# Cached keys prepared once per page and kept in DRAM, one score pass over 544 keys, masks kept in DRAM

## What is computed

```python
# layer 0: B=32 rows, S=32 tokens, HID=512, D=128, 32 query heads, 8 key heads
q, k, v = x @ Wq.T, x @ Wk.T, x @ Wv.T              # per head of 128
q, k    = rope(rmsnorm(q) , pos), rope(rmsnorm(k), pos)
kc, vc  = k_cache[block_table], v_cache[block_table]  # 16 pages of 32 tokens per row: 512 cached keys
scores  = q @ concat(kc, k).T / sqrt(D)               # 512 + 32 keys
scores  = where(key_index < seqlens or key is new, scores, -1e30)
x       = x + (softmax(scores) @ concat(vc, v)) @ Wo.T
# layer 1: x = x + x @ W.T + 2 * sum over the two best of 8 experts of gate * (x @ A.T) @ B.T
```

## Time and profile before

| | |
|---|---|
| runs | 1477.67, 1478.95, 1482.95 us; median 1478.95 |
| profiled execution, span from first to last instruction | 1451.3 us (the profile gives no own time beside its span; the median of the runs is 27.7 us above it) |
| PE busy (matmul) | 1356.5 us, 93% |
| DVE, ACT, POOL busy | 78%, 53%, 67% |
| mean granted TensorE clock | 0.982 of full speed |
| DMA moved | 188.72 MB, mean 130 GB/s |

### The profile page before, as it was taken

One profiled execution on the slowest core, in us unless ns is written; L12 is line 12 of the kernel. 1 busy time (PEld: TensorE's weight loads), 2 busy tenths in 40 slices (PEclk: granted clock), 3 DMA queues, 4 the chain that ended last, 5 costly groups with the idle time before them and its releaser, 6 DMA issues.

```text
span 1451.3 us, 28498 instructions
## 1 busy us (share of the span) xinstructions
PE 1356.5 (93%) x8640; PEld 1162.0 (80%) x8640; DVE 1132.6 (78%) x2891; ACT 766.9 (53%) x1989; POOL 973.1 (67%) x1269
## 2 busy tenths in 40 slices
PE   2599999998999999999999999999999999999889
PEld 1478888887878888887777888888787888888777
DVE  6688877777887778788877878887888888777754
ACT  1356555555664555556554555666555556555431
POOL 5676777777766677776766777777777777676500
PEclk8699999999999999999999999999999999999999
DMA  6434444454543343436533433445544343435401
GB/s 228 133 87 121 133 119 134 123 173 133 173 117 116 125 119 125 135 108 202 164 117 107 138 112 112 128 125 181 170 142 129 104 129 117 131 122 167 124 22 58
DMA packets 61380, 188.72 MB, mean 130 GB/s; under 512 B 10736, under 2 KB 11504, under 8 KB 58608
## 3 DMA queue, kind: packets, MB, share of 16 engines
q0 software_dynamic: 40960, 134.25, 31.3%
q1 hardware_dynamic: 19504, 53.50, 10.5%
q10 hardware_dynamic: 864, 0.46, 0.1%
HBM read 177.95 MB, written 12.32 MB: 131 GB/s over the span
## 4 chain that ended last, share of the span: by engine, by line
PE 69%; DVE 21%; issue 5%; ACT 2%; DMA 1%; DVEq 1%; POOL 0%; SPq 0%; ACTq 0%; POOLq 0%
PE PROJ L182 13%; PE MISC L182 13%; PE O L359 10%; PE S L182 10%; PE PT L349 8%; PE KT L338 5%; DVE probs L736 4%; PE O L361 3%; DVE scores L729 2%; PE PROJ L328 2%; DVE kT_lo L750 2%; DVE rope_v L703 2%; PE PROJ L330 2%; DVE mask L716 2%; DVE rope_u L699 2%
## 5 line engine op out<-in xcount | busy, mean ns | idle before, releaser
L976 POOL DMA_INDIRECT kv_rows<-in_kv,step_idx x512 | 529.8, 1035 | 219.6 <-issue 117.8
L550 ACT ACTIVATE pT<-PT 128x640 f32<-128x640 f32 x256 | 180.2, 704 | 300.6 <-PE PT L349 300.6
L359 PEld LDWEIGHTS O<-pT,kv_rows 128*128 128x128 f32 x2048 | 262.6, 192 | 27.0 <-ACT pT L550 9.8
L359 PE MATMUL O<-pT,kv_rows 128*128 128x128 f32 x2048 | 274.8, 277 | 2.9 <-ACT pT L550 2.6
L546 ACT ACTIVATE kT_hi<-KT 128x512 fp32r<-128x512 f32 x256 | 151.2, 590 | 225.1 <-PE KT L338 225.0
L750 DVE TENSOR_TENSOR kT_lo<-KT,kT_hi 128x512 fp32r<-128x512 f32 x256 | 176.0, 687 | 71.3 <-ACT kT_hi L546 70.7
L554 ACT ACTIVATE probs<-scores,min_all 128x640 f32<-128x640 f32 x256 | 212.7, 831 | 23.3 <-DVE min_all L729 21.0
L349 PEld LDWEIGHTS PT<-ident,probs 128*128 128x128 f32 x1280 | 142.1, 141 | 89.9 <-DVE probs L736 78.7
L349 PE MATMUL PT<-ident,probs 128*128 128x128 f32 x1280 | 191.3, 280 | 22.7 <-DVE probs L736 22.3
L729 DVE CUSTOM_DVE_ANT_0 scores<-S,mask,min_new 128x512 f32<-128x512 f32 x256 | 190.5, 744 | 0.0
L182 PE MATMUL PROJ<-w_hi,x_hi 128*128 128x512 f32 x384 | 172.0, 448 | 15.0 <-DVE w_lo L663 12.6
(11 more groups left out here) (215 smaller groups left out, 2702.6 us busy)
## 6 DMA issues: line engine op xcount, KB each, us to landing
stage<-in_wqkv SPq DMA_DIRECT2D x12, 1024.0 KB, 7.7
x_raw<-in_xT SPq DMA_DIRECT2D x32, 256.0 KB, 4.2
stage<-in_wo SPq DMA_DIRECT2D x8, 1024.0 KB, 6.6
kv_rows<-in_kv,step_idx POOLq DMA_INDIRECT x512, 3.7
y_tile<-y_running SPq DMA_DIRECT2D x32, 256.0 KB, 3.7
y_running<-y_tile SPq DMA_DIRECT2D x31, 256.0 KB, 2.1
out<-kv_rows SPq DMA_DIRECT2D x8, 256.0 KB, 2.0
stage<-in_w1T SPq DMA_DIRECT2D x1, 1024.0 KB, 6.7
```

The costliest lines, as they stand in the source:

```text
L359: nc.tensor.matmul(O[:, 0:P], kv_rows[:, b, c, GK * D + h * D:GK * D + (h + 1) * D], pT[:, c * P:(c + 1) * P], start=c == 0, stop=False)
L550: nc.scalar.activation(pT[:, :], PT[:, 0:KEYS], ACT.Copy).then_inc(sm["pT_ready"], 1)
L976: G.indirect_dma_start(kv_rows[:, b, c, :], None, kv[:, :], bass.IndirectOffsetOnAxis(ap=step_idx[:, b * LC + c:b * LC + c + 1], axis=0)). ...
```

## The change

Keys are turned and split once per page and group, not once per use. A unit is 8 pages (256 keys) of both heads: PE turns it with four transposes (turn_unit), ACT rounds it, DVE takes the rest, and SP stores it in a DRAM tensor kT_pages, 64 KB for a page with both parts and both heads (128 partitions x 512 B). The units of group 0 are made at the start, those of group g+1 during group g. For each batch row SP reads 16 page numbers from the table into registers and issues 16 DMAs, one a page, into kT (load_pages). POOL gathers only the values (the count of gathers stays, each row is 1 KB and no longer 2 KB). [...] new_scores, the copy of the new scores and the fourfold wider probability tail are gone (the exponent and the normalisation run over 544). The masks are made once, kept in DRAM in bf16 and loaded twice a tile by a broadcast DMA. The weights pass through stage in halves of 512 KB, 10 a group, and are split in other places.

```diff
+    kT_dram = nc.dram_tensor("kT_pages", (GROUPS * PAGES, D, 2 * GK * PSIZE), F32, kind="Internal").ap()
+    mask_dram = nc.dram_tensor("mask_rows", (BATCH, KEYS), BF16, kind="Internal").ap()
...
-KEYS = L + P
+KEYS = L + SEQ
...
+            def load_pages(i, g, t, b):
...
+                sp.wait_ge(sm["s_done"], (i - 1) * PAIRS + b * GK + GK)
+                sp.nop(nofuse=True)
+                sp.reg_load(page, pages[0:1, bass.ds((t * ROWS + b) * NPP, NPP)])
+                for j in range(NPP):
+                    row = sp.snap(page[j], min_val=0, max_val=PAGES - 1)
+                    sp.dma_start(kT[:, b, j, :, :, :].rearrange("p z h s -> p (z h s)").bitcast(F32),
+                                 kT_dram[bass.ds(g * PAGES + row, 1), :, :].rearrange("a d n -> d (a n)")
+                                 ).then_inc(kT_in[b], 16)
...
             def body(g, t, final):
...
+                sp.wait_ge(sm["y_stored"], (i + 1) * 16)
+                sp.nop(nofuse=True)
                 sp.dma_start(y_tile[:, :], y_rows[bass.ds(t, 1), :, :].rearrange("a p n -> p (a n)")
                              ).then_inc(sm["y_in"], 16)
...
+                    load_pages(i + 1, gn, tn, 0)
+                if not (final and fixed and t >= TILES - 2):
+                    load_x(i + 2, (t + 2) % TILES if fixed else t + 2)
...
+                    load_pages(i + 1, gn, tn, 1)
+                    load_mask(i + 1, tn, 0)
...
+                        store_unit(n_unit + t + 1, g + 1, t + 1, False)
+                        if not fixed or t < TILES - 2:
+                            load_kn(n_unit + t + 2, g + 1, t + 2)
...
+                    load_pages(i + 1, gn, tn, 2)
...
+                    load_pages(i + 1, gn, tn, 3)
+                    load_mask(i + 1, tn, 1)
...
                 sp.wait_ge(sm["y_added"], CREDIT + i + 1)
                 sp.nop(nofuse=True)
                 sp.dma_start(y_rows[bass.ds(t, 1), :, :].rearrange("a p n -> p (a n)"), y_tile[:, :]
                              ).then_inc(sm["y_stored"], 16)
-                sp.wait_ge(sm["y_stored"], (i + 1) * 16)
-                sp.nop(nofuse=True)
...
+            def turn_unit(ps, src):
+                for h in range(GK):
+                    for c in range(2):
+                        at = (h * 2 + c) * P
+                        tr = nc.tensor.transpose(ps[:, at:at + P], src[:, c, h * D:(h + 1) * D], ident[:, :])
+                tr.then_inc(sm["ku_done"], 1)
...
-            def turn_kv(i, p):
-                b, h = p // GK, p % GK
-                pe.wait_ge(kv_in[b], (i + 1) * 16 * LC)
-                for c in range(LC):
-                    tr = nc.tensor.transpose(KT[:, c * P:(c + 1) * P], kv_rows[:, b, c, h * D:(h + 1) * D], ident[:, :])
-                tr.then_inc(sm["kT_done"], 1)
...
             def score(i, p):
                 b, h = p // GK, p % GK
-                pe.wait_ge(sm["kT_ready"], i * PAIRS + p + 1)
-                products(S[p % 2][:, :], q_of(b, h), (kT_hi[:, :], kT_lo[:, :])).then_inc(sm["s_done"], 1)
...
+                if h == 0:
+                    pe.wait_ge(kT_in[b], (i + 1) * 16 * NPP)
+                q_hi, q_lo = q_of(b, h)
+                for k, (j0, j1) in enumerate(parts_of_score(p)):
+
+                    pe.wait_ge(sm["min_ready"], n + 1 + k)
+                    k_hi, k_lo = (kT[:, b, j0:j1, z, h, :] for z in range(2))
+                    at = SX_AT[p % 2] + j0 * SEQ
+                    mm = three_pass(SX[:, at:at + (j1 - j0) * SEQ], lambda c: (q_hi, q_lo), lambda c: (k_hi, k_lo), 1, 0, 0)
+                mm.then_inc(sm["s_done"], 1)
...
-                rest_kT(i, 1)
-                make_mask(t * ROWS + 1, 1)
...
+                    u = unit_at(t, p)
+                    if u is not None and not final:
+                        rest_unit(UNITS + g * UNITS + u, MISC[:, :], k_split)
```

More of the change, by code:

```diff
@@ L429, in _ @@
-            with pe.Fori(0, TILES - 1) as t:
-                body(GROUPS - 1, t, True)
-            body(GROUPS - 1, TILES - 1, True)
+                    score(i + 1, 1)
+                project_out(i, 1, g * HALVES + WO_FIRST + 2)
+            walk(pe, body)
             def turn_y(t):
@@ L555, in exponent, with round_half @@
+                nc.scalar.activation(probs[:, p % 2, 0:KEYS], scores[:, p % 2, :], ACT.Exp, bias=min_all[:, p:p + 1],
                                      scale=-1.0, accum_out=den[:, p:p + 1]).then_inc(sm["exp_done"], 1)
-            def round_group_weights(g, t, p, final):
-                for m in range(SPLITS):
-                    own = m >= NBLK
-                    first = SPLIT_HI_AT[m]
-                    if (t, p) not in (first, (first[0], first[1] + 1)) or (final and not own):
+            def round_half(n, m, hi, src):
+                act.wait_ge(sm["stage1_in" if m % 2 else "stage0_in"], (n // 2 + m // 2 + 1) * 16)
+                nc.scalar.activation(hi, src, ACT.Copy).then_inc(sm["w_hi_ready"], 1)
@@ new lines, in round_weights, with startup_halves @@
+                    round_half(group * HALVES, m, half_parts(m)[0], stage[:, m % 2, :, :])
+                for m in range(4):
+                    if final and (t, p) == L1_HI_AT[m]:
+                        act.wait_ge(sm["proj_done"], GROUPS * TILES * NBLK - NBLK + max(m - 1, 0) + 1)
+                        round_half(GROUPS * HALVES, m, l1_parts(m)[0], l1_stage(m))
+            def startup_halves(m):
+                for m in (m, m + 1):
+                    round_half(0, m, half_parts(m)[0], stage[:, m % 2, :, :])
@@ new lines, in startup_unit @@
+            def startup_unit(u):
+                take_unit(u, wide[u % 6], unit_split(u, True), True)
+            startup_halves(0)
+            for u in range(4):
+                startup_unit(u)
+            take_block(0, 0)
+            square_block(0, 0)
+            startup_halves(2)
+            for u in range(4, UNITS):
+                startup_unit(u)
+            sines(0, slice(0, 1))
+            startup_halves(4)
+            take_block(0, 1)
+            square_block(0, 1)
+            take_block(0, 2)
@@ new lines, in rest_weights @@
+            def rest_weights(g, t, p, final):
+                for m in range(HALVES):
+                    own = m >= WO_FIRST
+                    if (t, p) != LO_AT[m] or (final and not own):
+                        continue
+                    hi, lo = half_parts(m)
+                    rest_half((g if own else g + 1) * HALVES, m, lo, hi, stage[:, m % 2, :, :])
+                for m in range(4):
+                    if final and (t, p) == L1_LO_AT[m]:
+                        hi, lo = l1_parts(m)
+                        rest_half(GROUPS * HALVES, m, lo, hi, l1_stage(m))
```

860 lines of the change are left out of this document (473 added, 387 removed).

## The result

| | before | changed |
|---|---|---|
| median of the runs, us | 1480.44 | 1830.82 (1829.36 to 1836.97, 4 runs) |
| ratio to before | | 1.2397 (95% interval 1.237 to 1.2424) |
| span of the profiled execution, us | 1451.3 | 1828.6 |
| mean granted TensorE clock | 0.982 | 0.874 |

The change costs 350 us. The forecast was 1725, in a range of 1550 to 1860.

The account below looks back on a forecast made before the run. PE bounds the kernel before; after the change SP's instruction issue does. Start 97, 31 tiles with units and weights 1535 and end 70 make a span of 1702; plus 27.7, rounded to 1725 us, range 1550 to 1860.

Parts of the forecast that it names:

- A page load 0.55 us: SP's queue: register operations, move, DMA and gaps for one page take 0.55 us; 64 make 34.9 us a tile.
- A register load 1.5 us: SP's queue: reading 16 page numbers from SBUF into registers takes 1.5 us; four a tile, 6.0 us (0.4 to 9.2).
- The chance of 0.12: Chance given to register loads on SP of over 2.3 us each.
- Store to load of y_tile 2.6 us: SP at a tile's end: store of y_tile, its landing and loop end until y_tile's load take 2.6 us, nothing issued.
- A tile without a unit 46.6, with one 49: SP's sum for a tile: page loads 34.9, register loads 6.0, rest 5.7; a unit's store and key load add 2.9 us.
- 31 bodies 1535: SP from first to last loop body: 31 tiles of 46.6, plus 70 for units and 20 for weights, 1535 us.
- Start 97, end 70: Before SP's first body 97 us, with group 0's units and first pages; after the last y_tile store 70 us.
- +27.7 from the span to the runs: Added to the span of 1702: the median of runs lay 27.7 us above the span of before; gives 1730.
- PE would need 36.3 us: PE's program per tile after the change: 36.3 us, from 40.3, with key transposes and small score matmuls removed.
- SP keeps up: Rival: a page costs 0.44 us, a register load 0.1, so PE's 36.3 bounds; time near 1350; chance 0.06.
- A lower clock of PE, chance 0.03: Rival: PE's granted clock falls; chance 0.03.
- What would show it: PE waits for the transfer of kT first: Sign that the forecast is right: the transfer of kT leads PE's waits, with some 10 us a tile.

Follow-up runs that it names:

- e11: The changed kernel, unedited, run once more in a set where the kernel before took 1453.16 us; 1727.95 us, ratio 1.1897.
- e2: Against the changed kernel: the 16 page DMAs a row stay, with fixed addresses, no register loads and no register operations; 1583.0 us.
- e1: Against the changed kernel: each batch row's 16 page loads become one DMA with a constant address, no page-number lookup; 1475.29 us, ratio 0.9988.
- e3: Against the changed kernel: a tile's four register loads of page numbers dropped, the registers keep old numbers; 1737.47 us, ratio 1.176.
- e5: Against e1: the product of the new values takes all 128 rows, not 32 (adds products that don't belong); 1387.59 us, ratio 0.9541.
- e8: Against the kernel before: the product of the new values takes only its 32 rows, not 128, same sums; 1520.75 us, ratio 1.0284.
- e6: Against the changed kernel: y_tile's wait and load moved behind the first row's pages, row 2's 16 page loads sent from ACT; 1638.1 us, ratio 1.1252.

## Why the prediction was right, and where it wasn't

The forecast said slower by 17%, SP bound; it is 24% slower, and SP bound. Its steps are best read in the run at the level of its own trace, 1727.95 (e11). That the forecast of 1725 lies 3 us from it is luck: its sum of spans was 20 us short, and the 27.7 us added at the end didn't belong there, as shown below. That 1830.8 lies in the range is luck too, for the range reached up to 1860 for a dear register load, which the runs don't show, and not for a second level. The stores of y_tile in e11 run from 152.0 to 1644.8, and its first register load in the loop stands at 98.6.

- *PE bound before, SP's idle time spent.* Right: SP's wait for y_tile's sum fell from 1042.2 us to 43.7, and taking SP's work away gave back 248 us with the same packets (e2) and one DMA a row the whole loss (e1).
- *A page load 0.55 us.* Right in size: (8.41 - 0.33)/15 = 0.539 in e11, 64 of them 34.5 us for 34.9 (its parts, 0.551, times 64 are 35.3, so the recorded product is 0.4 too low). The parts don't simply add up, for without the register work e2 still has 0.47. At the upper level (9.26 - 0.33)/15 = 0.595 and (8.57 - 0.33)/15 = 0.549 in the tile shown.
- *The transfer is no bound, the issue is.* Right: e2 and the changed kernel move the same packets and differ by 248 us. A page takes SP 0.54 us, and by the queue's row in the profile after (228.79 MB in 42.7% of 1828.6 us) 0.22 us of the 16 engines.
- *A register load 1.5 us.* Too dear: its own duration is 0.97 us (row below), and leaving it out (e3) gave 0.75 each. By the prediction's own scale the 124 of them are 66 us less than it had.
```profile
L297 SPq TENSOR_LOAD <-pages x124: 968/974/2759, 98.6 to 1629.6; - x124
```
  The chance of 0.12 was for loads of over 2.3 us each. The longest of the 124 took 2.76 us, the median 0.97.
- *Store to load of y_tile 2.6 us.* Too cheap: 302.25 - 298.61 = 3.64 in e11.
- *A tile without a unit 46.6, with one 49.* The last group's inner tiles of e11, without units, are 45.6 to 45.9 apart, those with one 47.6 to 48.8. So a unit costs some 2.2 us for 2.9, and the errors above cancel in part (4 x 0.5 and 0.4 less, 1.0 more).
- *31 bodies 1535.* In e11 1644.8 - 98.6 = 1546. But 31 x 45.7 and 24 x 2.2 make 1470: the other 76 lie at the changes of group, where the sum had 20. The step that SP is late there, so that its waits for splits "are over when it comes to them, and cost nothing", failed: the tiles at a change are 55.4, 49.4 and 58.5 apart, and SP waits for splits (in e11 k_split 17.6 and w_lo 13.9 us). How the rest of the 76 divides isn't shown.
- *Start 97, end 70.* 98.6, and 1721.5 - 1644.8 = 76.7.
- *+27.7 from the span to the runs.* The step that failed most, and with it the forecast's distance to 1830.8. The sum of spans was 1702 for 1721.5 measured. The 27.7 us were taken for something that stays the same from kernel to kernel. They were the distance between two levels, for the profiled run of e11 took 1723.31 us, 1.8 above its own span, and that of the changed kernel 1830.48, 1.9 above its own. And the level isn't a constant: it cost the kernel that waits on SP's instructions 103 us, nearly four times the 27 that it cost the one that doesn't.
- *PE would need 36.3 us.* Right for what it counted: PE is busy for 35.6 in e5. But the cut of the new values' product from 128 rows to 32 was passed over as an edit without a price, and it costs 1.3 us a tile (e8). The *SP keeps up* rival at 1350 was therefore too low by a good deal: with SP's work gone the runs gave 1387.6 without the short product at the lower level, and 1475.3 with it at the upper one.
- *A lower clock of PE, chance 0.03.* The mean granted clock is 0.874 for 0.982. In the tile shown it was 1.00 of full speed, but 0.50 from 295 to 305 us, and PE stood for most of 291 to 297. PE's busy share of 78%, over the 65 to 75 forecast, comes from this in part: in the tile shown PE is busy for 41.8 us at 0.90, in e1's for 38.6 at 1.00 with about the same instructions. The short product is in both. In the inner tiles of e1, e5 and e6, where PE stops less, the granted clock is 1.00 again. It bound nothing, since SP's time doesn't hang on it.
- *What would show it: PE waits for the transfer of kT first.* Wrong in form. No wait of PE for the transfer of kT is shown. By the two rows below SP's lateness reached PE through the masks, which stand behind the pages in SP's queue, then DVE's scores, ACT's exponent and copies:
```profile
DVE scores L922 <- DMA mask<-mask_rows: 137.5, 27, 8.8
```
```profile
PE O L523 <- ACT pT L736: 284.5, 104, 15.3
```

No version tried here is the full computation and faster than before; the nearest is e6, at 1.125.

## What to carry to other kernels

Before moving work from a busy engine to many small DMAs, count the issuing queue's instructions: here 64 loads of 64 KB a tile cost 0.54 us each on one queue, and with them an inner tile takes 48 us (e11), where it took 40.3 before and takes 37.6 without them (e5, with the new values' product over 128 rows). Of the 355 us that one DMA a row gives back (e1), 16 DMAs a row with constant addresses give back 248 (e2): what was expensive is reading the page numbers and issuing by them, and not the transfers. And before adding a constant for "the runs against the trace", make sure that both are of one level: compare one run's own time with its own span.

## What was not expected of the hardware

- A product of 128x128 fp32 with operands of 32 rows took longer than one of 128 rows: 321 ns in e8 for 275 before (mean durations in the groups by line), and 42.7 us in 1520.75 by the runs of e8, where nothing else was changed.
- A load of 16 registers out of SBUF took SP 0.97 us at the median, and up to 2.8 (e11).
- Sixteen page loads a row moved in packets of 512 bytes, one DMA for the same sixteen pages in packets of 2048 (e1). And a page load's DMA instruction took 333 ns with register work between two of them and 432 without (e2).
- SP's small instructions have two levels from one set of runs to another: moves of 29 to 38 ns at the one, up to 733 ns at the other, with equal medians; 6% of a kernel that SP bounds. Both levels were seen on one chip.
- Page loads from two queues at once (e6) kept their pace in inner tiles: sixteen in 8.3 to 8.4 us on SP in a tile in which ACT sent sixteen more, as in e11 where SP sent them alone.
